# A decoder layer's mLSTM stage on one core: units of eight 128x128 blocks instead of two, mask added on TensorE, scores in 64-row groups

## What is computed

```
# per batch element and head (8 heads of 32 features), t = query, s = key
log_d = lf[t] - lf[s] + i_pre[s]        # lf: cumulative sum of log-sigmoid(f_pre)
log_d = where(t >= s, log_d, -inf);  m = max_s(log_d)
s_mat = (q @ k.T / sqrt(32)) * exp(log_d - m)
denom = max(abs(sum_s s_mat), exp(-m)) + 5e-5
h     = (s_mat @ v) / denom
h     = h * rsqrt(mean(h*h) + 1e-6) * gain
x     = x + h;  xn = layernorm(x);  logits = xn @ router_w + router_b   # softmax, top 2
```

## Time and profile before

| | us |
|---|---|
| median of 3 runs (lowest, highest) | 1127.43 (1127.26, 1127.62) |
| the profiled execution | 1128.98 |
| its span | 1127.2 |
| PE busy | 885.7 (79%) |
| DVE busy | 691.3 (61%) |
| POOL busy | 576.1 (51%) |
| ACT busy | 473.0 (42%) |
| mean granted clock of PE | 0.922 |

### The profile page before, as it was taken

The page is one execution under the profiler, slowest core; times in us unless marked ns, Lnnn a source line. Parts: engine busy times, 40 slices in busy tenths (PEclk is TensorE's granted clock), DMA queues, the critical chain, the costliest instruction groups (busy, mean ns, idle before and its releaser), DMA issues.

```text
span 1127.2 us, 31616 instructions
## 1 busy us (share of the span) xinstructions
PE 885.7 (79%) x11680; PEld 670.1 (59%) x11768; DVE 691.3 (61%) x1524; ACT 473.0 (42%) x842; POOL 576.1 (51%) x784
## 2 busy tenths in 40 slices
PE   5888999998982187677666640699999999999995
PEld 3566666665652065455444520578787787787874
DVE  4767776766652667787877873355555555555553
ACT  2656666665652153443443421233333333333331
POOL 2455565646552455677777775134434434344433
PEclk8999999998986598988999965799999999999998
DMA  8113334342335232333333323233333333333322
GB/s 260 39 40 70 110 77 123 74 123 69 90 96 149 78 114 69 114 112 104 115 118 108 103 88 113 72 49 50 49 50 49 50 49 50 49 49 51 48 40 24
DMA packets 130350, 92.48 MB, mean 82 GB/s; under 512 B 74176, under 2 KB 111168, under 8 KB 130080
## 3 DMA queue, kind: packets, MB, share of 16 engines
q1 hardware_dynamic: 116784, 72.10, 23.4%
q0 software_dynamic: 13296, 17.83, 9.5%
q10 hardware_dynamic: 128, 0.53, 0.2%
HBM read 54.38 MB, written 37.12 MB: 81 GB/s over the span
## 4 chain that ended last, share of the span: by engine, by line
PE 52%; DVE 13%; POOL 11%; ACT 9%; DMA 6%; issue 6%; SPq 1%; POOLq 1%; DVEq 0%; ACTq 0%
PE pair L807 17%; PE pair L820 9%; PE pair L822 7%; POOL sm L1387 4%; PE pair L568 4%; PE pair L554 3%; PE pair L532 3%; DVE SD L1006 2%; DMA o_scr<-On 2%; POOL SD L1379 2%; PE pair L581 2%; DMA STG<-wup_in 2%; POOL xs_scr L1395 1%; PE pair L778 1%; DVE hh L1040 1%
## 5 line engine op out<-in xcount | busy, mean ns | idle before, releaser
L807 PE MATMUL pair<-XTs,WU 128*128 128x128 bf16 x3408 | 285.4, 220 | 5.2 <-issue 2.7
L807 PEld LDWEIGHTS pair<-XTs,WU 128*128 x3408 | 239.2, 98 | 72.9 <-issue 8.6
L1420 POOL DMA_INDIRECT out_d<-XB x71 | 114.0, 1606 | 241.1 <-DVE XB L1150 223.2
L820 PE MATMUL pair<-WD,Hh 128*128 x480 | 181.5, 379 | 0.0
L1294 ACT ACTIVATE Hf<-pair 128x512 f32<-128x512 f32 x142 | 84.8, 597 | 224.4 <-PE pair L807 224.4
L1141 DVE CAST Hh<-Hf 128x512 bf16<-128x512 f32 x142 | 62.9, 443 | 177.1 <-ACT Hf L1294 177.1
L822 PE MATMUL pair<-WD,Hl 128*128 x568 | 154.9, 273 | 4.7
L1338 POOL TENSOR_SCALAR_AFFINE_SELECT PT<-PT 128x512 f32<-128x512 f32 (+1 forms) x96 | 74.4, 788 | 71.3 <-ACT PT L1179 62.8
L707 PE MATMUL pair<-QB,QC 128*128 128x256 bf16 (+1 forms) x768 | 87.2, 253 | 22.0 <-DVE SD L1006 21.2
L1143 DVE TENSOR_TENSOR Hl<-Hf,Hh 128x512 bf16<-128x512 f32 x142 | 99.8, 703 | 4.9
L1249 ACT ACTIVATE SD<-pair 128x512 f32<-128x512 f32 (+1 forms) x128 | 60.9, 492 | 98.4 <-PE pair L699 96.1
(11 more groups left out here) (217 smaller groups left out, 1824.5 us busy)
## 6 DMA issues: line engine op xcount, KB each, us to landing
XB<-xs_scr SPq DMA_DIRECT2D x71, 130.0 KB, 2.1
STG<-wup_in SPq DMA_DIRECT2D x32, 256.0 KB, 4.4
q_scr<-SPL SPq DMA_DIRECT2D x16, 512.0 KB, 4.0
STG<-wdn_in SPq DMA_DIRECT2D x32, 256.0 KB, 2.8
...
```

Source lines behind the costliest of these rows:

```text
L807: t = e.matmul(upb[r][k][:, 128 * (fm % 4):128 * (fm % 4) + 128], WU[:, bass.ds(reg[j] * 4096 + off, 128)], XTs[:, r, hx, dk, :], start=n ...
L820: e.matmul(yb[r][:, 0:512], Hh[:, r, hsl], WD[:, bass.ds(reg[i] * 4096 + 512 * fk, 512)], start=fk == 0, stop=False, skip_group_check=True)
L1420: e.indirect_dma_start(out=out, out_offset=bass.IndirectOffsetOnAxis(ap=XS[:, i % NX, 256:257].bitcast(I32), axis=0), in_=Yf[:, i % NY, :] ...
```

## The change

The mLSTM stage is rewritten, with what feeds it.

- *Units.* A block has three units in place of eight, steps `D` and `S`: unit 0 has the four heads of the first feature half with keys 0 to 127, unit 1 those of the second half, unit 2 all eight heads with keys and queries from 128. Each is eight 128x128 blocks, 128x1024 elements. Gates fill the PSUM pair `ZD` and scores the pair `ZS`, and there is one of each. SD has three buffers.
- *Mask.* Two matmuls per unit write the mask (mkb, -1e30 above the diagonal) to ZD before the gates are added. POOL's select is gone.
- *Row groups.* LR (gates) and QB (queries) hold two heads in each half of the 128 rows, kept apart by zeros, and each matmul contracts over 64 rows; g = 0 and 1 write different banks.
- *Sums.* `B3` now squares `ob` and copies `den` apart, and six small float32 matmuls (L753, L755) sum over the features and pick the denominators. The scaling by 1/sqrt(32) and the gain is done as `ob` leaves PSUM (GN, now one column for each feature half).
- *LayerNorm's second pass* (`B5n`) is on ACT; the router's matmuls are float32, four in place of twelve.
- *Order.* `mlstm_steps` is new: PV of a block's second and third units comes in the next iteration, the norm and router steps are later by up to one iteration, and the list has two more iterations.
- *Loads.* Eight transfers for LR in place of two for LH and RH; QC, four of QB and CX are issued with them, all at step `B1`.
- *Gates stage.* G is stored so that it can be transposed without a copy (GT is gone), DVE clears LR and half of the WD region that QB and QC use, and POOL's two memsets of WD are gone.

```diff
 def mlstm_steps():
...
+    for i in range(B + 6):
...
+        for u in range(3):
+            if ok(i):
+                yield "D", i, u
+                yield "S", i, u
+            if u < 2 and ok(i - 1):
+                yield "PV", i - 1, u + 1
+            if u == 2 and ok(i):
+                yield "PV", i, 0
...
+            if u == 2:
+                if ok(i - 3):
+                    yield "B6", i - 3, 0
+                if ok(i - 4) and i % 2:
+                    yield "R4", i - 4, 0
+                if ok(i - 1):
+                    yield "B4", i - 1, 0
+                    yield "B4p", i - 1, 0
...
         def tensor_mlstm(e, w):
...
+                if kind == "D":
+                    un = UN[b, u]
+                    if un:
+                        w.wait_ge(te_.sem, te_.at(*us[un - 1]))
+                    w.wait_ge(lr_z, 1)
+                    w.wait_ge(l_lr[r], 128 * (b // 2 + 1))
+                    n = 2 if u < 2 else 4
+                    for g in range(2):
+                        e.matmul(ZD[:, g, :].rearrange("p (a c) -> p a c", a=n)[:, :, 0:128], mkb[:, :],
+                                 idb[:, :].rearrange("p (a c) -> p a c", a=1).broadcast_to([128, n, 128]),
+                                 start=True, stop=False, skip_group_check=True)
+                    for dk, st_, z0, t0, wd in heads(u):
+                        for a in range(2):
+                            for g in range(2):
+                                rows = slice(64 * g, 64 * g + 64)
+                                c = 256 * a + z0
+                                t = e.matmul(ZD[:, g, c:c + wd], LR[rows, r, 0, dk, 128 * st_:128 * st_ + 128], LR[rows, r, 1 + a, dk, t0:t0 + wd],
+                                         start=False, stop=True, skip_group_check=True)
                     t.then_inc(d_.sem, 1)
...
+                elif kind == "S":
+                    un = UN[b, u]
+                    if un:
+                        w.wait_ge(sd_.sem, sd_.at(*us[un - 1]))
...
+                                    t = e.matmul(ZS[:, g, c:c + wd], QC[rows, r, hc, dk, 128 * st_:128 * st_ + 128],
+                                                 QB[rows, r, a, hq, dk, t0:t0 + wd], start=n == 0, stop=n == 2, skip_group_check=True)
                     t.then_inc(s_.sem, 1)
...
         def vector_mlstm(e, w):
...
+                    e.tensor_tensor(SD[:, un % 3, :, :], ZS[:, :, :].rearrange("p g (a c) -> p (g a) c", a=2), SD[:, un % 3, :, :], ALU.mult).then_inc(sd_.sem, 1)
...
         def gpsimd_mlstm(e, w):
...
-                    e.affine_select(out=dg, in_=dg, pattern=[[0, 2], [1, 128]], compare_op=ALU.is_ge, fill=0.0, base=0,
-                                    channel_multiplier=-1).then_inc(sz_.sem, 1)
...
         def sync_mlstm(e, w):
...
+                w.wait_ge(s_.sem, s_.at(b - 2, 2))
+                w.wait_ge(lr_z, 1)
+                for j in range(4):
+                    hv = gsc[:, 8 * b:8 * b + 8, :].rearrange("q (k j) c -> q k j c", j=4)[:, :, j, :]
+                    e.dma_start(LR[32 * j:32 * j + 3, r, 0, :, :], hv[0:3]).then_inc(l_lr[r], 16)
+                    e.dma_start(LR[32 * j + 3:32 * j + 6, r, 1 + j % 2, :, :], hv[3:6]).then_inc(l_lr[r], 16)
```

More of the change, by code:

```diff
@@ L126, in mlstm_steps @@
 def mlstm_steps():
[L127 to L134 removed]
+    pend, ready, chunk, sent = [], 0, 36, 0
@@ L735, in tensor_mlstm @@
-                    lg_free(w, step)
+                        for dk in range(2):
+                            e.matmul(sums[:, tt, 4 * dk:4 * dk + 4], sq[:, 256 * dk + 128 * tt:256 * dk + 128 * tt + 128], CF[:, C_IN:C_IN + 4],
+                                     start=True, stop=True)
+                        t = e.matmul(sums[:, tt, 8:16], dn[:, 128 * tt:128 * tt + 128], CF[:, C_DN:C_DN + 8], start=True, stop=True)
+                    t.then_inc(dn_.sem, 1)
+                    w.wait_ge(hh_.sem, hh_.at(b - 1))
@@ L1604, in constants @@
     c[:, C_M1] = p % 32 >= 16
+    for j in range(4):
+        c[:, C_IN + j] = p // 32 == j
+        for k in range(2):
+            c[32 * j + k, C_DN + 4 * k + j] = 32.0 ** -0.5
     c[:, C_S0] = p % 32 < 2
```

490 lines of the change are left out of this document (208 added, 282 removed).

## The result

The changed kernel takes 1095.8 us (1095.6 to 1096.3, four executions) beside 1127.35 of the kernel before: ratio 0.9725, interval 0.9708 to 0.9741. In two later groups of runs the same kernel, unchanged, took 1086.3 and 1086.8 us, ratios 0.966 (0.963 to 0.969) and 0.9661 (0.9641 to 0.9681). Its fourteen executions lie between 1084.9 and 1096.3 us and those of the kernel before, over all groups, between 1120.4 and 1128.1; the 0.2% named in the prediction was too fine for either. The gain is 31.5 to 38 us where 65 were forecast.

A forecast was written before the change was run, and what follows sets the result against it. The mLSTM stage was taken to be bounded by DVE and POOL handing work to each other, 17.47 us per block. Stage -68, gates stage -1 and tail +4 gave -65 us: forecast 1062 us, range 1040 to 1098.

The forecast's parts named there:

- Tile-mode switches: PE in the mLSTM stage: switches rise from four to about nine per block, two on the path, 0.4 us.
- the rival reading: PE's tiling mode: every switch drains the engine and costs a full latency, making the sum that of rival B on PE.
- PE's sum: PE's work per mLSTM block after the change: about 9.3 us of the 11.9 before.
- the walk: One mLSTM iteration traced from the sums' arrival: even 11.6 us, odd 13.0, mean 12.3, with allowances 13.0 per block.
- The sums and the router on PE: Small float32 matmuls per mLSTM block: six for the sums take 0.8 us, the router's four 0.5.
- rival B: mLSTM stage: PE (64-row groups not overlapping) or SP's loads set a slower pace, 14.3 to 16.5 us per block; chance 0.24.
- DVE stalls against the weight split: mLSTM stage: what is left of DVE waiting beside POOL's weight split, 0.3 us per block.
- The first four blocks: Start of the mLSTM stage: lacking router work or followers, they take 7.5, 9.5, 10.5 and 11 us.
- Tail: After the last iteration's sums: eighteen scatters follow the statistics, 43.3 us against 39.6 before, +4.
- D: mLSTM stage slower than before: single buffers force full series, 21.5 us per block, about 1190 us; chance 0.04.
- E: Nothing gained: DVE and POOL hold each other at the old pace through `pow` and scatters, 1125 to 1130; chance 0.02.
- The likeliest case: mLSTM stage: the walk holds, 11.8 to 14.3 us per block, 1047 to 1078 us; chance 0.60.

The follow-up runs named there:

- e2: Changed kernel plus seven filling bf16 matmuls on PE before the scores of unit 2, results unused; 1084.3 us, ratio 0.9655.
- a0: The changed kernel, unchanged, run again as a yardstick; 1086.3 us, ratio 0.9660.
- a1: The changed kernel, unchanged, run again as the yardstick of another group; 1086.8 us, ratio 0.9661.
- g5: Changed kernel with early loads, fourteen filling matmuls before scores 2, and both the six sums and the router's logits in bf16; 1064.2 us, ratio 0.9465.
- h3: Changed kernel with early loads, reordered stage start and POOL's new order together, float32 matmuls kept; 1070.5 us, ratio 0.9515.
- h5: h4 plus seven filling matmuls on PE before the scores of unit 2; 1044.2 us, ratio 0.9289.
- h4: h3 with the six sums in bf16, their low parts left out; 1053.2 us, ratio 0.9373.
- h2: Changed kernel with POOL's order alone altered: weight split moved ahead of `pow`, two of four scatters per even iteration behind it; 1071.6 us, ratio 0.9537.

## Why the prediction was wrong

Its range held the time, its size didn't: the stage lasts 229 us (first gates at 389 to the sums' arrival of iteration 15 at 618) where 194.5 were forecast. Of the 34.5 us, 8 lie before the first sums, 2 in the next two iterations and 24 in the twelve that were walked at 13.0. At full clock and with no late start those twelve would take about 13.85 each (e2 below), 10 of the 24; the other 14 are clock, loads and late signals in the first profile (12 and 4 us in a0 and a1). By its own steps:

- *Products, exp, POOL's select, DVE's tail, LayerNorm on ACT*: right. DVE after the sums went as walked: product 1 ends 8.8 us after them in even iterations (walked 8.6).
- *64-row groups*: right, 0.82 to 0.84 us for a unit's scores (0.68 and latency).
- *Tile-mode switches*: 0.4 us for the two on the path, right in size. From the last scores' start to the first PV's it is 0.15 us, from the last PV's to the router's first 0.31, where starts within scores or PV lie 0.03 apart. Whether each switch costs a full latency, as the rival reading had it, stays open: 0.15 is under the 0.22 that the prediction takes for one, and 0.31 is over it.
- *PE's sum*: the terms listed come to 8.4 us, 8.9 with the second set of transposes, not the 9.3 named; the walk doesn't use it.
- **The sums and the router on PE**: the failed term. "The sums' six small matmuls ... take 0.8" and "the router's four likewise 0.5": 1.34 and 0.91 at full clock, and up to 2.6 and 1.7 at half. They stand on the path in every iteration. In e2, even iterations at clock 1.00 take 13.1 and odd ones 14.6, mean 13.85; in g5 the even one is 11.0. Mis-sized by 0.95 us per block, 14 us in the stage. Taking nearly all of their 2.25 us away gave 13 us alone and 19 with early loads, and the sums alone 17 beside h3: more than was mis-sized, less than the 30 us that 2 us per block would be, since the odd iterations then wait for `pow`. Even the upper bound, L733's 0.15 each, was too low: L733 are transposes, which leave one record each, where these leave two, and come to 0.22 to 0.23 each.
- **PE's clock**: not a term at all. The walk used durations at full clock, since the stage had 0.93 before, though the new order leaves PE idle for 2.2 us before scores 2. It has 0.80 to 0.85, and each fall in an odd iteration costs up to 2.6 us. Above e2's 13.85 the three profiles have 0.6 to 1.6 us per block, with the waits for loads and the late starts in it. That a half-clock share does cost time is shown by h5 (1.00, 12.03 us) against h4 (0.93, 12.48); how much of the changed kernel's own 15 is clock alone was not separated from loads and late starts.
- *Loads*: rival B's doubt about "half a microsecond of room" was right; scores 0 waited 0.4 to 1.7 us in ten of the fifteen odd iterations of the three profiles. Taking the wait away gave nothing that could be measured alone.
- *DVE stalls against the weight split*: allowed 0.3, measured, in the first profile, 1.03 in each odd iteration on the tensor_scalar and 0.24 in even ones on the add, 0.6 per block.
- **The first four blocks**: walked 7.5 + 9.5, and the sums of block 0 come after 25 us; 8 us too late, of which h2 gives back 5 to 7, ACT's wait for the weight chunk. The walk had no SP queue in iteration 0, where 28 transfers stand ahead of the chunk.
- *Gates stage* -1: -1.9. *Tail* 43.3 after iteration 15's sums: 44.6. *Attention*, not foreseen: 2.2 us shorter. The sum of all these, 1062 + 34.5 + 1.3 - 0.9 - 2.2, is 1094.7, beside 1095.8 measured first. This is a sum of stretches and no account of causes.
- *Rivals*: the time lay in B, by neither of B's two mechanisms alone. D and E did not come near.

The likeliest case had the right mechanism for DVE and POOL, and lost by three terms on other engines: one priced from another kind of matmul, one not priced at all, and one walked without SP's queue. That the time still fell into the range is no merit of these terms; the range was wide enough for all three.
